# Maxima of the second attention: turned by VectorE and carried through a DRAM buffer, and the order of work at the seam of two stages

## The reference

```python
x = x + attn_a(layernorm(x))   # 16 heads of 64: softmax(Q K^T / 8) V, exact gelu, Wpost, its own residual
x = x + ffn(layernorm(x))      # relu(x W1q + b1) W2q + b2, W1q and W2q of -1, 0, 1 (threshold from mean |W|)
x = x + attn_b(layernorm(x))   # 16 heads of 16, biases, rotary positions on q and k, softmax, wo
x = x + ffn(layernorm(x))
```

## Time and profile before

| | us |
|---|---|
| median of 3 runs | 3825.49 (3824.11 to 3829.05) |
| profiled execution, its own time | 3828.33 |
| its span | 3826.2 |
| PE busy | 3658.7 (96%) |
| DVE busy | 2724.2 (71%) |
| ACT busy | 2318.7 (61%) |
| POOL busy | 1927.7 (50%) |

### The profile page before, as it was taken

How to read it: one execution, slowest core, us unless ns; L and a number is a source line. 1 busy time by engine, 2 the same in 40 slices (tenths; PEclk the granted TensorE clock), 3 DMA queues, 4 the chain that set the end, 5 groups by cost and what they waited for, 6 DMA issues and landing times.

```text
span 3826.2 us, 64594 instructions
## 1 busy us (share of the span) xinstructions
PE 3658.7 (96%) x23938; PEld 2458.9 (64%) x23938; DVE 2724.2 (71%) x4335; ACT 2318.7 (61%) x4501; POOL 1927.7 (50%) x1218
## 2 busy tenths in 40 slices
PE   8999999999999999999999868999999999999987
PEld 5777777777777777777777554555555555555534
DVE  6766667667666666766667757888888888887772
ACT  5666656565565656656665435666666666666654
POOL 4555555555555555555555443455555555554412
PEclk9999999999999999999999988999999999999998
DMA  2000000000000000000000022333333333333220
GB/s 78 7 12 1 12 12 12 1 12 12 1 12 12 12 1 12 12 1 12 12 4 12 24 47 51 53 58 58 58 58 62 57 59 59 56 57 57 51 46 17
DMA packets 90933, 114.15 MB, mean 30 GB/s; under 512 B 10752, under 2 KB 64384, under 8 KB 90624
## 3 DMA queue, kind: packets, MB, share of 16 engines
q1 hardware_dynamic: 90624, 110.02, 14.3%
HBM read 33.43 MB, written 25.17 MB: 15 GB/s over the span
## 4 chain that ended last, share of the span: by engine, by line
PE 82%; DVE 8%; POOL 4%; ACT 3%; issue 2%; SPq 0%; DMA 0%; DVEq 0%; POOLq 0%; ACTq 0%
PE ps_o L616 12%; PE ps_s L585 10%; PE ps_t L598 8%; PE ps_t L216 7%; PE ps_o L692 6%; PE ps_t L727 5%; PE ps_m L598 4%; PE ps_s L665 4%; PE ps_t L718 4%; PE ps_t L223 4%; PE ps_t L651 3%; PE ps_m L216 3%; DVE max_b L1090 3%; PE ps_s L679 2%; PE ps_m L718 2%
## 5 line engine op out<-in xcount | busy, mean ns | idle before, releaser
L485 POOL TENSOR_TENSOR e_a<-e_a,recip 128x1024 f32<-128x1024 f32 x512 | 969.7, 1894 | 959.4 <-DVE recip L956 959.3
L770 ACT ACTIVATE e_a<-ps_s,neg_max 128x512 f32<-128x512 f32 x1024 | 694.3, 685 | 554.2 <-DVE neg_max L949 553.8
L1090 DVE TENSOR_REDUCE max_b<-ps_s 128x2 f32<-128x1024 f32 x512 | 623.6, 1219 | 177.3 <-PE ps_s L665 175.5
L812 ACT ACTIVATE et<-ps_s 128x1024 f32<-128x1024 f32 x512 | 523.4, 1022 | 359.6 <-PE ps_s L679 359.0
L949 DVE TENSOR_REDUCE neg_max<-ps_s 128x2 f32<-128x1024 f32 x512 | 622.9, 1217 | 69.6 <-PE ps_s L585 69.6
L616 PE MATMUL ps_o<-et_a,v_a 128*64 128x256 f32 x4096 | 500.4, 386 | 7.0 <-DVE heads_a L992 1.8
L585 PE MATMUL ps_s<-raw_a 64*128 64x512 f32 x3072 | 428.3, 411 | 11.2 <-ACT e_a L770 11.1
L517 POOL TENSOR_TENSOR h_lo<-h,h_hi 128x512 fp32r<-128x512 f32 x256 | 330.2, 1304 | 178.0 <-ACT h_hi L856 178.0
L598 PE MATMUL ps_t<-ident,e_a 128*128 128x128 f32 x2660 | 395.0, 281 | 7.7 <-DVE xl L1137 5.8
L616 PEld LDWEIGHTS ps_o<-et_a,v_a 128*64 128x64 f32 x4096 | 279.6, 137 | 190.3 <-issue 76.6
L963 DVE COPY et_a<-ps_t 128x512 f32<-128x512 f32 x366 | 251.0, 688 | 204.1 <-PE ps_t L598 200.0
(11 more groups left out here) (196 smaller groups left out, 7323.5 us busy)
## 6 DMA issues: line engine op xcount, KB each, us to landing
q_stack<-roped_q SPq DMA_DIRECT2D x256, 64.0 KB
k_stack<-roped_k SPq DMA_DIRECT2D x256, 64.0 KB
x_a<-X SPq DMA_DIRECT2D x16, 512.0 KB, 3.8
X<-x_a SPq DMA_DIRECT2D x16, 512.0 KB, 2.9
x_ahead<-X SPq DMA_DIRECT2D x16, 512.0 KB, 3.8
X<-x_ahead SPq DMA_DIRECT2D x16, 512.0 KB, 4.3
q_stack<-roped_q SPq DMA_DIRECT2D x256, 32.0 KB
k_stack<-roped_k SPq DMA_DIRECT2D x256, 32.0 KB
```

Of the source, the lines that this page charges most:

```text
L485: nc.gpsimd.tensor_tensor(e_a[:, u % 5, :, :], e_a[:, u % 5, :, :], factor, ALU.mult).then_inc(e_normed, 1)
L770: ins = nc.scalar.activation(e_a[:, u % 5, h, :], ps_s[:, 2 * (u % 2) + h, :], ACT.Exp, bias=neg_max[:, u % 5, h:h + 1], accum_out=sums[:, ...
L812: nc.scalar.activation(et[:, v % 5, :, :], ps_s[:, 2:4, :], ACT.Exp)\
L1090: nc.vector.reduce_max(max_b[:, u // 4 % 2, :, u % 4], ps_s[:, score_bank(u):score_bank(u) + 2, :], AX.X, negate=True).then_inc(max_done, 1)
```

## The change

1. The maxima of a pair no longer pass PE, ACT and a shared bank. DVE does three instructions in a row, each waiting for the one before: high part (copy, 128 by 8), low part (subtract, 128 by 8), and a transposition in squares of 32 by 32 of 128 by 32 (`turn_max`, step 8p + 9). SP writes the result to a small DRAM buffer M1 (`save_max`, step 8p + 10), waits until it has landed, and reads it back with two DMAs into `q_stack` (`max_rows`, step 8p + 12).
2. The ones in `k_stack` come from a small tile by two DMAs (`load_key_ones`), not from a memset of 128 by 4096 on DVE.
3. At the seam: quantising w1 goes from slot 504 to 505, w2 from 506 to 512; the split of WB from 508 and 509 to 514 and 515; the memset of `v_b` from 514 to 516; the last four products with Wpost from slots 525 to 528 to slots 536 to 538, and the save of x behind them. What needs their buffers waits for them (`stack`, `parts_high`).
4. For the first ffn of sequences 0 and 1, every second `h_lo` is made by DVE (`first_hidden_low`).

```diff
-        ones = at("ones", 150, [P, P])
+        ones = at("ones", 1.5, [P, P])
-        POST, LAST_POSTS = ((32, 32, 35, 36), (43, 44, 51, 52)), (45, 46, 47, 48)
+        POST, LAST_POSTS = ((32, 32, 35, 36), (43, 44, 51, 52)), (56, 57, 58, 58)
-        RESIDUAL, LOAD_X, SAVE_X, LAST_SAVE = 13, -22, 54, 50
+        RESIDUAL, LOAD_X, SAVE_X, LAST_SAVE = 13, -22, 54, 60
-        LOAD_W, LOAD_WB, LOAD_REST, SPLIT, ABS = 40, 484, 503, (508, 509), (471, 473)
-        GAMMA, QUANTISE, SCALE, CLEAR = 474, (504, 506), 514, (513, 514)
+        LOAD_W, LOAD_WB, LOAD_REST, SPLIT, ABS = 40, 484, 503, (514, 515), (471, 473)
+        GAMMA, QUANTISE, SCALE, CLEAR, KEY_ONES = 474, (505, 512), 513, 516, 523
-            plan += [(8 * p + 9.25, "max", "attn", p, s) for p in range(PAIRS)]
+        def low_by_dve(n):
+            return n % 2 == 1 and n in first_ups
+        first_ups = {nth_up["ffn0", f, s] for f in range(FT) for s in range(2)}
...
                 def stack(s, pair):
+                    if s == 0 and pair == 0:
+                        wait_filled(sp, fill_of["post", 1, TB - 1, BATCH - 1])
...
-                    if s == 0:
-                        sp.wait_ge(ones_set, 1)
+                def load_key_ones():
+                    sp.wait_ge(weights_ready, 2)
+                    sp.wait_ge(weights_split, 2)
+                    sp.wait_ge(gamma_ones, 1)
+                    for h in range(2):
+                        sp.dma_start(k_stack[64 * h + 48:64 * h + 50, :, :].bitcast(F32).rearrange("p a s -> p (a s)"),
+                                     ones[64 * h:64 * h + 64, :]).then_inc(key_ones_in, 16)
+                def save_max(s, pair):
+                    sp.wait_ge(max_turned, PAIRS * s + pair + 1)
+                    if s or pair >= 2:
+                        sp.wait_ge(max_in[(pair - 2) % PAIRS], 2 * 16 * (s + (pair >= 2)))
+                    sp.dma_start(M1[pair % 2, :, :].rearrange("r (q c) -> q r c", q=4), m_turned[:, pair % 2, :]).then_inc(max_out, 16)
                 def max_rows(s, pair):
-                    wait_emptied(sp, fill_of["max", "attn", pair, s])
-                    for part in range(2):
-                        sp.dma_start(q_stack[48 + part:P:64, pair, :].bitcast(F32), m_rows[0:8, pair % 2, part, :].bitcast(F32))\
-                            .then_inc(max_in[pair], 16)
+                    sp.wait_ge(max_out, 16 * (PAIRS * s + pair + 1))
+                    for h in range(2):
+                        rows = M1[pair % 2, 0:16, :].rearrange("(p h t) c -> h p (t c)", p=2, h=2)[h, :, :]
+                        sp.dma_start(q_stack[64 * h + 48:64 * h + 50, pair, :].bitcast(F32), rows).then_inc(max_in[pair], 16)
...
-                    elif kind == "max":
-                        pe.wait_ge(max_done, UNITS * s + 4 * i + 4)
-                        last = nc.tensor.transpose(bank(fill)[0:8, 0:P], max_b[:, i % 2, :, :].rearrange("p h t -> p (h t)"),
-                                                   ident[:, :])
...
-                    elif kind == "max":
-                        wait_filled(act, fill)
-                        if s or i >= 2:
-                            act.wait_ge(max_in[(i - 2) % PAIRS], 2 * 16 * (s + (i >= 2)))
-                        nc.scalar.activation(m_rows[0:8, i % 2, 0, :], bank(fill)[0:8, 0:P], ACT.Copy).then_inc(m_high, 1)
...
                 def parts_high(i, half, s):
+                    if s == 0 and half == 0:
+                        if i == 0:
+                            act.wait_ge(parts_ready, PAIRS * BATCH)
+                        else:
+                            wait_filled(act, fill_of["post", 1, TB - 1, BATCH - 1])
...
-                def set_key_ones():
-                    dve.wait_ge(a_qk_done, UNITS_ALL)
-                    nc.vector.memset(k_stack[:, :, :].bitcast(F32), 1.0).then_inc(ones_set, 1)
+                def turn_max(s, pair):
+                    n = PAIRS * s + pair
+                    dve.wait_ge(max_done, 4 * n + 4)
+                    if n == 0:
+                        dve.wait_ge(m_set, 1)
+                    if n >= 2:
+                        dve.wait_ge(max_out, 16 * (n - 1))
+                    exact, parts = max_b[:, pair % 2, :, :].rearrange("p h t -> p (h t)"), m_parts[:, pair % 2, :]
+                    link(nc.vector.tensor_copy(parts[:, 0:8], exact))
+                    link(nc.vector.tensor_tensor(parts[:, 8:16], exact, parts[:, 0:8], ALU.subtract))
+                    nc.vector.transpose(m_turned[:, pair % 2, :], parts.bitcast(F32)).then_inc(max_turned, 1)
+                def first_hidden_low(part, i, s):
+                    n = nth_up[part, i, s]
+                    dve.wait_ge(hi_copied, n + 1)
+                    nc.vector.tensor_tensor(h_lo[:, i, :], h32[:, n % 4, :], h_hi[:, i, :], ALU.subtract).then_inc(first_low, 1)
```

More of the change, by code:

```diff
@@ L349, in hybrid_block_kernel, with wait_low @@
         nth_up = {(part, i, s): n for n, (_, kind, part, i, s) in enumerate(x for x in plan if x[1] == "up")}
+        def low_by_dve(n):
+            return n % 2 == 1 and n in first_ups
+        first_ups = {nth_up["ffn0", f, s] for f in range(FT) for s in range(2)}
+        lows_before = [0]
+        for n in range(2 * FT * BATCH):
+            lows_before.append(lows_before[-1] + (0 if low_by_dve(n) else 1))
+        def wait_low(engine, n):
+            if low_by_dve(n):
+                engine.wait_ge(first_low, n + 1 - lows_before[n + 1])
+            else:
+                engine.wait_ge(h_split, lows_before[n + 1])
         x_of = {"ffn0": x_ahead, "attn": x_ahead, "ffn1": x_before}
@@ L462, in _ @@
                         load_rest()
+                    if slot == KEY_ONES:
+                        load_key_ones()
                     for step in (2 * (slot - SHIFT), 2 * (slot - SHIFT) + 1):
@@ L471, in _ @@
                                 stack(s, STACK.index(r))
+                            if r >= 10 and (r - 10) % 8 == 0 and (r - 10) // 8 < PAIRS:
+                                save_max(s, (r - 10) // 8)
                             if r >= 12 and (r - 12) % 8 == 0 and (r - 12) // 8 < PAIRS:
@@ L553, in _ @@
                         for kind, part, i, s, fill in steps_of.get(step - 3, []):
-                            if kind == "up":
+                            if kind == "up" and not low_by_dve(nth_up[part, i, s]):
                                 hidden_low(part, i, s)
@@ L722, in product @@
                             if i == 0:
-                                pe.wait_ge(h_split, nth_up[part, f, s] + 1)
+                                wait_low(pe, nth_up[part, f, s])
                             if part == "ffn0" and s == 0 and f == 0 and i == 0:
@@ L1039, in set_value_ones @@
                     nc.vector.memset(v_b[:, :, :, :, HB:32], 1.0).then_inc(ones_set, 1)
+                    nc.vector.memset(m_parts[:, :, 16:32].bitcast(F32), 0.0).then_inc(m_set, 1)
                 def scale_biases():
@@ L1174, in _ @@
                             empty_low(*todo)
+                        for kind, part, i, s, fill in steps_of.get(step - 3, []):
+                            if kind == "up" and low_by_dve(nth_up[part, i, s]):
+                                first_hidden_low(part, i, s)
                         if step % 2 == 0 and 0 <= step // 2 < UNITS_ALL:
                             unit_max(step // 2)
+                        if step % 8 == 1 and 9 <= step < 2 * UNITS_ALL + 8:
+                            turn_max((step - 9) // SLOT, (step - 9) % SLOT // 8)
                         for piece, part, s in norm_steps.get(step, []):
@@ L1204, in _ @@
                         scale_biases()
-                    if slot == CLEAR[0]:
-                        set_key_ones()
-                    if slot == CLEAR[1]:
+                    if slot == CLEAR:
                         set_value_ones()
@@ L1245 @@
     x1 = nc.dram_tensor("X1", arrays["X"].shape, mybir.dt.float32, kind="Internal").ap()
+    m1 = nc.dram_tensor("M1", (2, 32, 128), mybir.dt.float32, kind="Internal").ap()
     out = nc.dram_tensor("OUT", arrays["X"].shape, mybir.dt.float32, kind="ExternalOutput").ap()
[L1247 removed]
+    hybrid_block_kernel(nc, *args, x1, m1, out)
     r = run_bass_kernel_spmd(nc, [arrays], core_ids=[0])
```

32 lines of the change are left out of this document (16 added, 16 removed).

## The result

| | before | after |
|---|---|---|
| median (of 4 runs each, same chip) | 3824.8 (3818.4 to 3829.1) | 3886.1 (3877.6 to 3887.9) |
| profiled execution, span | 3826.2 | 3886.1 |
| first up product | 2200.75 | 2191.61 |
| first score product of attn_b | 2282.27 | 2273.24 |
| from there to the last matmul | 1539.4 | 1608.0 |

After over before is 1.0149, interval 1.0136 to 1.0162. The forecast was 3811, its range 3790 to 3838, with 0.16 on slower. The seam came out near the forecast as a sum (9.0 us earlier instead of 12), though not term by term. The whole loss lies in the second stage: 68.6 us, where the forecast had a gain of 2.

The account below looks back on a forecast made before the run. PE, busy 96% of the span, was taken to set the pace, DVE at 81% not far behind. From 3828.3, 2 us off the second stage and 12 off the seam gave 3814.3, as a median 3811, range 3790 to 3838.

Parts of the forecast that it names:

- Three at 0.18 and two short waits are 0.6 us.: Second stage, DVE: the new three-instruction chain for a pair's maxima takes 0.6 us, bounds 0.4 and 1.2.
- It reaches PE only where the next maximum is late already: one in nine.: Second stage: DVE's added time delays PE only at 56 waits among 493 maxima, costing 4 us (0 to 42).
- 16 us: Second stage: gain from taking 128 transpositions off PE, 80 of them counted as free; bounds 13 and 25.6.
- The way through DRAM, 10 us: Second stage, pair 5's maxima: PE stalls 1.0 us in each of 15 sequences, leaving a 10 us loss (0 to 50).
- W: Time from issue to landing of the maxima's write to DRAM, taken as 1.75 us; bounds 1.6 and 2.9.
- The first rival: Second stage: the round trip through DRAM decides, slower, 3841 us with a write landing in 2.6 us; chance 0.18.
- The seam, 12 us: Between the stages: four terms, 12 - 4.7 + 3 + 1.6, sum to a gain of 12 us, bounds 0 and 20.
- (a): Seam: w2 and WB preparation moved behind slot 511 brings the first up product 12 us earlier, bounds 7 and 12.2.
- (b): Seam, first ffn: the moved work delays sequence 0's low parts and tile 0's down products, -4.7 us (0 to -8).
- (c): Seam: queries rotated 7 us earlier leave POOL out of the way of DVE's normalisations, gain 3 us (0 to 6).
- (d): Seam: sequence 1's low parts shared between POOL and DVE end earlier, gain 1.6 us, bounds 0 and 3.
- One sign that the forecast gave for being wrong: Second stage: PE waiting for maxima much more than 56 times would show DVE's share was taken too small.

Follow-up runs that it names:

- one_turn: Changed kernel with the maximum written straight into the tile that is turned, without DVE's copy and subtraction, low part zero: 3818.0 us, ratio 0.9972 to the kernel before.
- three_turns: one_turn with DVE's transposition of the maxima made three times in a chain: 3848.8 us, ratio 1.0054 to the kernel before.
- seven_turns: one_turn with DVE's transposition of the maxima made seven times in a chain: 3911.0 us, ratio 1.0215 to the kernel before.
- pe_twice: Changed kernel with the maxima's old way and PE's transposition of them made twice: 3818.7 us, ratio 0.9976 to the kernel before.
- turn_row: one_turn with one row and one read, no row for the low part: 3819.2 us, ratio 0.9977 to the kernel before.
- pool_parts: Changed kernel with copy and subtraction on GpSimd, DVE only turning, one step later: 3853.3 us, ratio 1.0065 to the kernel before.
- posts_back: Changed kernel, maxima's old way, last four Wpost products and save of x back in their old slots: first score product at 2273.94 us, no total given.
- weights_back: Changed kernel, maxima's old way, preparation of w2 and WB and memset of v_b back in their old slots: first score product at 2279.73 us, no total given.
- lows_back: Changed kernel, maxima's old way, all low parts of the first two ffns on GpSimd again: first score product at 2274.79 us, no total given.

## Why the prediction was wrong, step by step

- **"Three at 0.18 and two short waits are 0.6 us."** The step that failed first. It is right for a chain that nobody holds (shortest 0.58), but the chain took 1.69 on average, since copy and subtraction run SBUF to SBUF beside POOL's 1.3 us instructions. The rows it was sized by were no guide: over the whole trace of before the reciprocal took 252 to 256 ns and the transposition 695 to 712, never held. A better one stood in the prediction, used for the seam alone: the low parts of keys at 1456 ns, twice what the same shape takes for queries. The groups of before, then of after:

```profile
L1086 DVE TENSOR_TENSOR roped_q<-q_rot,roped_q 128x512 fp32r<-128x512 f32 x32 | 23.8, 743 | 0.0
```

```profile
L1116 DVE TENSOR_TENSOR roped_k<-k_rot,roped_k 128x512 fp32r<-128x512 f32 x32 | 21.8, 682 | 0.3 <-ACT roped_k L903 0.3
```

  In after neither is held, and the keys' low parts take 682 ns. Without the held chain the waiting is back, but not always at the same place: in one_turn keys take 1401 and queries 790, in three_turns 708 and 1421. So which small instruction is held depends on where it falls beside GpSimd's, and a mean of one kernel needn't hold for the next.
- **"It reaches PE only where the next maximum is late already: one in nine."** The second failure. three_turns and seven_turns measured one half for unheld work, at 0.49 and at 1.48 us alike; after gives 68 us for 191, 0.36. DVE's maximum and PE's score product form a loop with one pair of banks, in which a delay may soon find no slack; why it is one half no run shows. Even the weight load's waits (123) would have given only one in four. The measured chain with one in nine would be 128 x 1.42 / 9 = 20 us instead of 4, so the first step alone does not make the loss.
- **"16 us" for PE's transpositions.** Near nothing: pe_twice, turn_row and one_turn agree. 96% busy was read as "sets the pace", but PE's order contains the loop through DVE, and a shorter order only waits longer. The forecast named this effect and still took 80 transpositions of 123 as free, with 67 as the least.
- **The way through DRAM, 10 us.** The mechanism is there in pool_parts (15 waits, all at pair 5). W was 2.5 at pair 5 and not 1.75, and in after it cost next to nothing (one wait of 1.6 us from 2300 to 3700), hidden behind the other waits. In one_turn it stood in 5 waits of 4.9 us together. The first rival therefore priced a slower kernel (3841) for the wrong reason. It also speaks of "96 KB of copies" ahead of the write; that is one head's queries, and the sixteen copies are eight of 64 and eight of 32 KB, 768 KB.
- **The seam, 12 us.** 9.0 came. (a) 9.1 to the first up product, not 12. (b) -4.7 for tile 0: the first down product lost 3.7 of it, but by another way, a bank whose release stood behind the split of WB, and that behind DVE's wait for its first low part. The single pieces were shorter than forecast: WB's took 2.12 and 2.88 us there instead of 3.40 and 5.21, and `h_lo` 0.68 to 1.37; until the last down product of sequence 0 only 1.9 us were lost. (c) 3 us: the stretch to sequence 1's first up product became 1.8 us longer instead of shorter. The queries are rotated 7.5 us earlier, but the normalisations come 7.5 us earlier too, behind the same `rstd`, so they still run beside GpSimd. In after they take 5.0 us, not 2.32:

```profile
2232.83 2.66 DVE L1098 TENSOR_SCALAR xn<-x_ahead,mean_var,rstd 128x256 f32<-128x256 f32 x2 [1.13 <-POOL rstd L543]
2235.74 2.34 DVE L1098 TENSOR_SCALAR xn<-x_ahead,mean_var,rstd 128x256 f32<-128x256 f32 x2
```

  What makes the stretch longer is not shown: undoing any one part of the seam (posts_back, weights_back, lows_back) gives back 1.3 to 1.4 us of it. (d) 1.6 us: 3.6 from sequence 1's first up product to its last down product. That 9.0 came close to 12 is in part luck: (a) and (c) fell short by 7.7 us, and (b) and (d) made up 4.8 of them.
- **Rivals.** The one on the slower side was the DRAM path; a held DVE was not among them. That left 0.16 on slower, and a range whose upper end stood on W alone. One sign that the forecast gave for being wrong did come: waits for maxima well over 56, namely 100.

What was not settled: why the factor is one half at both lengths, and how much of after's 68 us is the clock. The granted clock from 2400 to 3500 is 0.97 in after against 0.99 and 1.00 in one_turn; PE stood waiting more often there. No run parts the two.

## What to carry to other kernels

Before putting a small copy or a subtraction from SBUF to SBUF on VectorE, look what GpSimd does at that moment: bound its time by the GpSimd instructions beside it, not by its size, and look for a group with the same form whose mean and minimum are far apart. Where PE and DVE hand one pair of banks to and fro, don't price DVE's time by the share of late waits; in this kernel about one half of it was on the path. Test it by repeating a harmless instruction, as three_turns and pe_twice did. PE at 96% is not proof that PE time is worth anything.

## What the runs showed of the hardware

- A VectorE copy or subtraction of 128 by 8 from SBUF to SBUF took 129 and 166 ns alone and up to 2078 and 2303 ns beside GpSimd (after); a transposition in squares of 128 by 32, also from SBUF to SBUF, took 210 to 215 ns in all 128 cases, directly behind them. The same copy on GpSimd took at most 663 ns (pool_parts).
- A PE that was 96% busy, with 25.6 us of work added: +0.9 us (pe_twice).
- From the issue of a write of 16 KB to DRAM in pieces of 128 bytes to SP's next instruction, which waits for it, there were 1.94 to 2.0 us where little stood ahead of the write, 2.5 behind sixteen copies and 4.0 behind a save of 512 KB (after). The Trainium skill (DMA: Bandwidth & Descriptors, section "Anatomy of one DMA — SWDGE (gpsimd) path") has a fixed cost of about 2.0 us, for transfers that GpSimd issues; these are issued by SP, which the forecast did not say. The forecast took 1.75, near the 1.6 us of a load of 2 KB, and 2.0 was nearer.
